# A step loop of an LSTM: the input's gate rows put into the sum by TensorE instead of added behind it

## What is computed

```python
def _lstm_activate(gates, c):
    i, f, g, o = jnp.split(gates, 4, axis=-1)
    c_new = jax.nn.sigmoid(f) * c + jax.nn.sigmoid(i) * jnp.tanh(g)
    h_new = jax.nn.sigmoid(o) * jnp.tanh(c_new)
    return (h_new, c_new)
def step(carry, x_t):
    h, c = carry
    logits = concatenate([h, c, x_t]) @ W_sel.T + b_sel
    s = argmax(logits)
    g = x_t @ W_ih[s].T + h @ W_hh[s].T + b_ih[s] + b_hh[s]
    h2, c2 = _lstm_activate(g, c)
    return ((h2, c2), h2)
```

## Time and profile before

| what | value |
|---|---|
| runs | 6276.47, 6270.70, 6274.82 us; median 6274.8 |
| the profiled execution | 6278.15 us, its span 6276.3 us |
| PE busy | 5392.8 us (86% of the span), 84948 instructions |
| DVE busy | 3097.9 us (49%), 13265 instructions |
| ACT, POOL busy | 1088.6 us (17%), 612.9 us (10%) |
| L1456, gate products | 59904 instructions, 1233.0 us |
| L1427, products that nobody reads | 4992 instructions, 1297.0 us |
| L1480, reductions | 1872 instructions, 670.0 us |
| L1486, additions of the input | 1872 instructions, 416.0 us |

### The profile page before, as it was taken

One profiled execution on the slowest core, in us unless ns is written; L12 is line 12 of the kernel. 1 busy time (PEld: TensorE's weight loads), 2 busy tenths in 40 slices (PEclk: granted clock), 3 DMA queues, 4 the chain that ended last, 5 costly groups with the idle time before them and its releaser, 6 DMA issues. The chain is left out here.

```text
span 6276.3 us, 214043 instructions
## 1 busy us (share of the span) xinstructions
PE 5392.8 (86%) x84948; PEld 3269.5 (52%) x84948; DVE 3097.9 (49%) x13265; ACT 1088.6 (17%) x4645; POOL 612.9 (10%) x1014
## 2 busy tenths in 40 slices
PE   8998778849998929999999999999999999977778
PEld 6643443314666615555555555555555555544444
DVE  4401443214552165555555555555555555564543
ACT  0000000002331131111111111111111111122312
POOL 0000660002650000000000000000000000011100
PEclk9999998979999969999999999999999999989877
DMA  0000111467432330000000000000000000000010
GB/s 10 21 30 11 39 44 44 97 136 253 119 105 100 139 123 5 5 5 10 5 5 5 10 5 5 5 5 10 5 5 5 5 10 0 0 24 37 23 55 9
DMA packets 128787, 240.28 MB, mean 38 GB/s; under 512 B 47084, under 2 KB 64114, under 8 KB 127687
## 3 DMA queue, kind: packets, MB, share of 16 engines
q1 hardware_dynamic: 68584, 146.72, 6.6%
q0 software_dynamic: 60128, 92.58, 5.9%
HBM read 165.58 MB, written 73.29 MB: 38 GB/s over the span
## 5 line engine op out<-in xcount | busy, mean ns | idle before, releaser
L1456 PE MATMUL bank<-lstm_w,step_h_parts 128*32 128x128 f16 (+1 forms) x59904 | 1233.0, 238 | 172.1 <-issue 164.0
L1456 PEld LDWEIGHTS bank<-lstm_w,step_h_parts 128*32 128x32 f16 x59904 | 1116.8, 97 | 488.4 <-issue 478.0
L1427 PE MATMUL bank<-lstm_w 128*128 128x512 f16 x4992 | 1297.0, 383 | 3.2 <-issue 3.2
L1480 DVE TRANSPOSE_TENSOR_REDUCE step_summed<-bank 128x4 f32<-128x128 f32 x1872 | 670.0, 358 | 292.7 <-PE bank L1456 285.6
L1427 PEld LDWEIGHTS bank<-lstm_w 128*128 128x128 f16 x4992 | 386.4, 98 | 388.5 <-issue 5.1
L1406 ACT ACTIVATE step_act_out<-step_gates 128x4 f32<-128x4 f32 x625 | 128.5, 206 | 2082.3 <-DVE step_gates L1486 2078.8
L1486 DVE SCALAR_TENSOR_TENSOR step_gates<-step_summed,lstm_inv_scale,step_xgs 128x4 f32<-128x4 f32 x1872 | 416.0, 222 | 68.7
L1530 DVE COPY step_xgs<-step_xg 128x16 f32 x624 | 109.2, 175 | 688.7 <-issue 664.5
L1396 POOL COPY xnT<-step_state 128x4 f32 (+1 forms) x625 | 116.4, 186 | 3170.0 <-DVE step_state L1513 3170.0
L1109 PE MATMUL bank<-sum_parts,sum_hot 125*125 125x512 f16 x1600 | 347.6, 381 | 6.9 <-DVE sum_parts L1068 6.9
L1437 PE MATMUL bank<-lstm_wsel,step_state 128*1 128x4 f32 x4992 | 214.9, 168 | 115.3 <-DVE step_state L1503 115.3
(11 more groups left out here) (368 smaller groups left out, 6578.2 us busy)
## 6 DMA issues: line engine op xcount, KB each, us to landing
rel_h<-rel_h_sb SPq DMA_DIRECT2D x39, 1024.0 KB, 4.3
lstm_xg<-xg_g POOLq DMA_DIRECT2D x4, 5000.0 KB, 19.5
step_xg<-lstm_xg SPq DMA_DIRECT2D x25, 800.0 KB, 4.4
xg_w<-in_c_w_ih SPq DMA_DIRECT2D x8, 2048.0 KB, 10.7
lstm_w<-in_c_w_hh SPq DMA_DIRECT2D x4, 4096.0 KB, 30.8
rel_z<-rel_z_sb POOLq DMA_DIRECT2D x8, 1250.0 KB, 22.9
rel_zg<-rel_z POOLq DMA_DIRECT2D x8, 1248.0 KB
cheb_w<-in_L_gnn_weight SPq DMA_DIRECT2D x8, 1024.0 KB
```

The source lines that it names most:

```text
L1427: nc.tensor.matmul(idle[:], w[:, 0, 0, 0, 0, 0:128], w[:, 0, 0, 0, 0, :], start=True, stop=True)
L1456: last = nc.tensor.matmul(bank[32 * q:32 * q + 32, 0:32 * (end - first)], h_parts[:, c, :], w[:, s, c, q, a, 32 * first:32 * end], start=( ...
L1480: nc.vector.tensor_reduce(summed[:, first:end], bank[:, 0:32 * (end - first)].rearrange("p (b r) -> p b r", r=32), X_AXIS, ALU.add, apply_ ...
```

## The change

It does four things.

1. `lstm_inputs` is turned: tiles of 125 steps by 512 gate values (16 groups of gate and cell, five tiles each, 80 in all), four products of 512 columns each. ScalarE and VectorE split each tile into three bf16 parts (high, middle, low), whose sum is the fp32 value; GpSimd stores each tile (three parts, 375 rows of 1 KB). The sum of the biases is split in the same way and stored once. The 16 weight loads have 1 MB.
2. In the loop there are four banks, one per gate, each with a column range per cell. For each gate TensorE runs one product (`inject`): a constant 0/1 matrix times the scale as stationary operand, the ring row of the step as moving operand (48 rows of inputs, 48 of biases, 512 columns). It starts the bank's sum; the gate products of the picked cell (128, all of 128 columns) are added to it. The rows for f and g are put in at the top of the loop, those for i and o behind the score products, in front of the wait for the pick. The additions L1486, the row copy L1530 and the buffer `gates` go; ScalarE reads `summed` and multiplies by `L.inv`. VectorE's reductions read the bank at a column offset taken from the pick.
3. `keep_clock_up` and all its products go.
4. VectorE's loop is `choose(t)` and then `finish(t)`, so that its jump back lies between h and the maximum. Four semaphores of the banks are counted down in `choose`. The wait for `h_kept` moves from in front of the cell state to in front of h. The input ring has three slots of five steps.

The diff, without the declarations and the bias splitting:

```diff
-CHUNK = 25
-RING = 3 * CHUNK
-
+GATES = 4
+XG_CHUNK = 5
+XG_SLOTS = 3
+XG_RING = XG_SLOTS * XG_CHUNK
+XG_ROWS = GATES * 4 * 3
...
-    B.xg = nc.dram_tensor("lstm_xg", (CELLS, 128, STEPS * GC), F32, kind="Internal").ap()
...
+    B.xg = nc.dram_tensor("lstm_xg", (GROUPS, 3, STEPS, 512), BF16, kind="Internal").ap()
...
-            for s in range(CELLS):
-                pool.wait_ge(kept_a, GC * (s + 1))
-                pool.wait_ge(kept_v, GC * (s + 1))
-                pool.dma_start(B.xg[s], g[:, s % 2].rearrange("p t g -> p (t g)")).then_inc(stored[s % 2], 16)
-            for i in range(2):
-                pool.wait_ge(stored[i], 16 * (CELLS // 2))
+            for i in range(TILES):
+                n, m = i // NT, i % NT
+                pool.wait_ge(lo_ready, i + 1)
+                pool.dma_start(B.xg[n, :, m * R:(m + 1) * R, :].rearrange("a t g -> t a g"), parts[:, i % 8]
+                               ).then_inc(stored[i % 8], 16)
+            for k in range(8):
+                pool.wait_ge(stored[k], 16 * (TILES // 8))
 
...
+            for i in range(TILES):
+                n, m = i // NT, i % NT
+                if m == 0:
                     pe.wait_ge(w_loaded[n % 2], 16 * (n // 2 + 1))
-                if i >= 4:
-                    pe.wait_ge(kept_a, i - 3)
-                    pe.wait_ge(kept_v, i - 3)
+                if i >= 6:
+                    pe.wait_ge(rest_ready, i - 5)
                 for c in range(KC):
-                    wt = w[:, n % 2, c, i % (GC // 2), :]
-                    nc.tensor.matmul(B.bank[2 * (i % 4)][:, 0:CUT], wt, xnT[:, c, 0:CUT], start=(c == 0),
-                                     stop=(c == KC - 1))
-                    last = nc.tensor.matmul(B.bank[2 * (i % 4) + 1][:, 0:N - CUT], wt, xnT[:, c, CUT:N],
+                    last = nc.tensor.matmul(B.bank[i % 6][0:R, :], xnT[:, c, m * R:(m + 1) * R], w[:, n % 2, c, :],
                                             start=(c == 0), stop=(c == KC - 1))
...
+    part_f = (0, B.bank[0], done_f, summed_f)
+    part_g = (1, B.bank[1], done_g, summed_g)
+    part_i = (2, B.bank[2], done_i, summed_i)
+    part_o = (3, B.bank[3], done_o, summed_o)
+    parts = (part_f, part_g, part_i, part_o)
+    score = B.bank[4][0:1, 0:8]
+    halves = [(c, a) for c in range(KC) for a in range(2)]
     with ExitStack() as here:
-        xg = sb("xg", [128, CELLS, RING * GC], F32)
-        xgs = sb("xgs", [128, GC], F32)
+        xg = sb("xg", [128, XG_RING, 512], BF16)
...
+            def load(k, slot):
+                sp.dma_start(xg[0:XG_ROWS, bass.ds(slot * XG_CHUNK, XG_CHUNK), :],
+                             xg_rows[:, bass.ds(k * XG_CHUNK, XG_CHUNK), :]).then_inc(xg_loaded, 16)
+
+            sp.dma_start(rows_f[:], I["c_xg_rows"]).then_inc(rows_loaded, 16)
+            sp.wait_ge(cleared, 1)
+            sp.dma_start(xg[64:64 + XG_ROWS, :, :], bias_rows.to_broadcast((XG_ROWS, XG_RING, 512))
+                         ).then_inc(bias_loaded, 16)
+            for slot in range(XG_SLOTS):
+                load(slot, slot)
+                sp.wait_ge(xg_loaded, 16 * (slot + 1))
+            with sp.Fori(XG_SLOTS, STEPS // XG_CHUNK) as k:
                 sp.wait_ge(init, 1)
                 sp.wait_ge(xg_loaded, k * 16)
-                sp.wait_ge(xgs_ready, (k - 2) * CHUNK)
-                sp.dma_start(xg[:, :, bass.ds((k % 3) * (CHUNK * GC), CHUNK * GC)],
-                             B.xg[:, :, bass.ds(k * (CHUNK * GC), CHUNK * GC)].rearrange("s p g -> p s g")
-                             ).then_inc(xg_loaded, 16)
-            sp.wait_ge(xg_loaded, STEPS // CHUNK * 16)
+                sp.wait_ge(injected, (k - (XG_SLOTS - 1)) * XG_CHUNK - 1)
+                load(k, k % XG_SLOTS)
 
...
-                act.wait_ge(gates_f, n)
-                nc.scalar.activation(act_out[:, 0:4], gates[:, 0:4], ACT.Sigmoid).then_inc(sig_f, 1)
-                act.wait_ge(gates_ig, n)
-                nc.scalar.activation(act_out[:, 4:8], gates[:, 4:8], ACT.Sigmoid).then_inc(sig_i, 1)
-                nc.scalar.activation(act_out[:, 8:12], gates[:, 8:12], ACT.Tanh).then_inc(tanh_g, 1)
+                act.wait_ge(summed_f, n)
+                nc.scalar.activation(act_out[:, 0:4], summed[:, 0:4], ACT.Sigmoid, scale=L.inv[:, 0:1]
+                                     ).then_inc(sig_f, 1)
+                act.wait_ge(summed_g, n)
+                nc.scalar.activation(act_out[:, 4:8], summed[:, 4:8], ACT.Tanh, scale=L.inv[:, 0:1]
+                                     ).then_inc(tanh_g, 1)
+                act.wait_ge(summed_i, n)
+                nc.scalar.activation(act_out[:, 8:12], summed[:, 8:12], ACT.Sigmoid, scale=L.inv[:, 0:1]
+                                     ).then_inc(sig_i, 1)
                 if ahead:
                     nc.scalar.copy(input_score[:], L.lx[:, bass.ds(n * CELLS, CELLS)]).then_inc(input_score_ready, 1)
-                act.wait_ge(gates_o, n)
-                nc.scalar.activation(act_out[:, 12:16], gates[:, 12:16], ACT.Sigmoid).then_inc(sig_o, 1)
+                act.wait_ge(summed_o, n)
+                nc.scalar.activation(act_out[:, 12:16], summed[:, 12:16], ACT.Sigmoid, scale=L.inv[:, 0:1]
+                                     ).then_inc(sig_o, 1)
                 act.wait_ge(c_ready, n)
                 nc.scalar.activation(tc[:], state[:, 0:4], ACT.Tanh).then_inc(tc_ready, 1)
 
...
-            def keep_clock_up(products):
-
-                for _ in range(products):
-                    nc.tensor.matmul(idle[:], w[:, 0, 0, 0, 0, 0:128], w[:, 0, 0, 0, 0, :], start=True, stop=True)
+            def inject(part, at, stop):
+                p, bank, _, _ = part
+                return nc.tensor.matmul(bank[:], rows[:, p, :], xg[:, at, :], start=True, stop=stop)
+
+            def add_half(part, s, c, a, stop):
+                p, bank, _, _ = part
+                for q in range(4):
+                    last = nc.tensor.matmul(bank[32 * q:32 * q + 32, 128 * s:128 * s + 128], h_parts[:, c, :],
+                                            w[:, s, c, q, a, 128 * p:128 * p + 128], start=False, stop=stop,
+                                            tile_position=(0, 32 * q))
+                return last
+
+            def cell(s):
+                for part in parts:
+                    for c, a in halves:
+                        last = add_half(part, s, c, a, stop=(c == KC - 1 and a == 1))
+                    last.then_inc(part[2], 1)
 
             pe.wait_ge(init, 1)
+            pe.wait_ge(rows_ready, 1)
+            pe.wait_ge(bias_loaded, 16)
+            pe.wait_ge(xg_loaded, 16)
+            for part in parts:
+                inject(part, slice(0, 1), stop=True).then_inc(part[2], 1)
             with pe.Fori(1, STEPS) as t:
 
-                pe.wait_ge(init, 1)
-                pe.wait_ge(input_score_ready, t)
+                pe.wait_ge(xg_loaded, (t // XG_CHUNK + 1) * 16)
+                at = bass.ds(t % XG_RING, 1)
+                for part in (part_f, part_g):
+                    pe.wait_ge(part[3], t)
+                    inject(part, at, stop=False)
+                pe.wait_ge(input_score_ready, 1)
+                pe.sem_inc(input_score_ready, -1)
                 nc.tensor.matmul(score[:, 0:CELLS], B.ones[0:1, 0:1], input_score[:], start=True, stop=False)
                 pe.wait_ge(c_ready, t)
                 for k in range(KC):
@@ -1441,25 +1506,13 @@
                     last = nc.tensor.matmul(score[:, 0:CELLS], tc[:, k:k + 1], h_weight[:, :, k], start=False,
                                             stop=(k == KC - 1))
                 last.then_inc(score_done, 1)
-                keep_clock_up(WARM_PICK - 1)
-                pe.wait_ge(init, 1)
+                for part in (part_i, part_o):
+                    pe.wait_ge(part[3], t)
+                    last = inject(part, at, stop=False)
+                last.then_inc(injected, 1)
+                pe.wait_ge(picked, 1)
                 pe.wait_ge(h_lo_ready, t)
-                keep_clock_up(1)
-                pe.wait_ge(picked, 1)
                 s = pe.value_load(pick[0:1, 0:1])
-
-                def cell(s):
-                    for first, end, bank, done, _, _ in parts:
-                        for c in range(KC):
-                            for a in range(2):
-                                for q in range(4):
-                                    last = nc.tensor.matmul(
-                                        bank[32 * q:32 * q + 32, 0:32 * (end - first)], h_parts[:, c, :],
-                                        w[:, s, c, q, a, 32 * first:32 * end],
-                                        start=(c == 0 and a == 0), stop=(c == KC - 1 and a == 1),
-                                        tile_position=(0, 32 * q))
-                        last.then_inc(done, 1)
-
                 with pe.If(s < 2):
                     with pe.If(s < 1):
                         cell(0)
@@ -1470,22 +1523,14 @@
```

(71 more changed lines are left out.)

159 lines of the change are left out of this document (88 added, 71 removed).

## The result

The changed kernel takes 6345.7 us in the median (6331.6 to 6365.0, 4 runs) where the kernel before takes 6274.6: ratio 1.0116, 95% interval 1.0082 to 1.015. It is slower by 71 us. The profiled execution took 6358.2, 12.5 over that median, with a span of 6356.4, 80.1 longer than before.

The account below looks back on a forecast made before the run. The prediction took the LSTM loop's serial chain, 5.16 us a step, as the bound. Steps gain 0.20 us and lose 0.39 to the clock: 624 x (-0.20 + 0.39) = +119, plus 6 around the loop, gives 6400 us; range 6145 to 6550.

Parts of the forecast that it names:

- the likeliest case: Whole kernel: TensorE's clock falls to half in some loop steps; 6400 us, own range 6240 to 6540, chance 0.52.
- Up to the state: Loop step, first gate product to cell state: 3.02 us falls to 2.47, a gain of 0.55 us a step.
- rival 4: Input additions weren't on the path, the jump back eats the rest, clock full: 6275 +- 12 us, chance 0.06.
- (a): Wait for kept h moves from cell state to new h, beside the tanh wait: 0.07 us, ends 0 and 0.09.
- (b): VectorE's jump back now on the path: maximum at least 0.37 us after the last half of h, before 0.08.
- (c): VectorE loses input-row copy and arithmetic, gains four decrements; reduction of f stays at about +0.8 to 1.0 us, hidden.
- (d): Score products already end before the maximum, so VectorE's jump back is last unless TensorE is late.
- rival 3: TensorE late with the score, 0.15 us a step: 6568 us with half clock in 0.3 of steps, 6250 full; chance 0.12.
- The clock: TensorE in the loop: half clock strikes 0.23 of the steps at 1.7 us each, +0.39 us a step.
- Rival 1: Clock stays full, four row products doing what eight dummies did: 6156 us, chance 0.30.
- The loop's end: Old profile after the last cell: TensorE idle 1.42 us, then half clock; taken as evidence that thin stretches lower the clock.
- Around the loop: Input stage, its stores, the loop's start and first passes: +6 us in sum, ends -15 and +25.

Follow-up runs that it names:

- two steps a pass: Changed kernel with VectorE's loop holding two steps between jumps back, TensorE and ScalarE unchanged: 6267.5 us.
- the wait alone: Changed kernel plus four dummies before the pick's wait (6241.2 us), with VectorE's wait for h_kept moved ahead of the reduction of f: 6222.9 us.
- the kernel with all of it mended: Changed kernel with all rows behind the score, h_kept wait ahead of f's reduction, two dummies directly behind the cell, eight steps per VectorE pass: 5953.0 us, ratio 0.948.

## Why the prediction came out as it did

The direction, the likeliest case and its mechanism were right: 6400 was forecast, 6345.7 came. Two terms of the sum were off, one by +50 us (the jump) and one by -94 (the clock). That the miss is 54 us and not 94 is luck: they partly cancelled.

- **Up to the state: right.** Reduction of o forecast at +2.04 and measured at 2.02, state +2.47 and 2.45 (means over the undisturbed steps; 2.21 and 3.03 before). The additions of the input had been on the path, so rival 4 is out; that is read from the traces, as no run takes them out alone. One price was left out: the scale of the activations, now a column in memory, holds 0.036 us of the path, hidden in a term that came out right.
- **(a) The wait for the kept h: right.** Forecast 0.07, measured 0.509 - 0.434 = 0.075; moving the wait took it away.
- **(b) The jump back: mechanism right, too small.** Forecast 0.37 from the last half of h to the maximum, measured 0.469 in every undisturbed step. The price was read from the old loop, where branch and first instruction behind it stood 0.19 us apart; in the new one they stand 0.30 apart, in every pass. Why the same kind of jump has different prices in the two loops no run shows. It is +0.10 a step, less the 0.02 by which the state came earlier: this is why the full-clock step is 5.04 and not 4.96, 50 us.
- **(c), (d):** the four decrements are hidden, as forecast. TensorE isn't last, but only just: with the jump gone, the maximum waits for the score and comes only 0.1 us earlier (two steps a pass showed it). So rival 3's late score exists, hidden behind the jump.
- **The clock: mechanism right, share and price too large.** Forecast 0.23 of the steps at 1.7 us each, +0.39 a step; measured 101 / 623 = 0.16 at 1.48, +0.24. That is 94 us less. The step from 4022.47 above costs the forecast's 1.70, the one from 4036.02 only 1.22 (6.26 us): there the clock fell after the cell had begun, and its reduction of f isn't late. The share was called the number that no row gives, and four dummies in place of eight in the old kernel, where the same amount streams, gave 148 of 623.
- **Rival 1 and the warning of gaps:** the clock didn't stay full. The largest idle gap of TensorE in the undisturbed step above is 0.79 us, the largest in all the loop's steps 1.36, and 101 steps had half clock all the same. The Trainium skill (TensorE: Matmul & The Clock Gate, Why this matters for your kernels) warns of longer gaps than these; read the other way round, as the prediction read it, that without them the clock stays full, it doesn't hold here. The loop's end, where the clock had fallen after 1.42 us, was the better witness.
- **Around the loop: right within 3 us.** The input stage's products run from 1902.4 to 2179.3, where they ran from 1909.1 to 2180.8: they start 6.7 us earlier (forecast 5) and take 5.2 longer (forecast 6), and the stage's tail is 2 shorter (forecast 5). So the next stage starts 3.5 us earlier (forecast 4), and the loop starts 9.7 later against that (forecast 10).
- **Instruction store:** the two instruction queues of the page of the profile moved 43 and 34 packets in the whole execution, 45 and 30 before, so nothing was reloaded from step to step. With the size that the Trainium skill (Runtime: NRT & Kernel Launch, Instruction fetch mechanics) gives for TensorE's store this agrees.

Terms: 624 x (+0.08 - 0.15) = -44 us and -3 around it, against 125 forecast: 78, the profiled difference of 80.

## What to carry to other kernels

Before dummy products are removed because real ones have come, count what TensorE streams between its dense bursts before and after, and run the old kernel with that many dummies: it prices the clock alone, in one run. Here it gave 141 us for the 150 of the changed kernel, though the number of half-clock steps and the price of one each came out otherwise (148 at 0.95, 101 at 1.48). When an operation is moved across a loop's end, the jump back moves onto the path with it (0.38 us here); holding a few steps in a pass takes it off again, as long as the code stays loaded (eight steps were fine, twelve cost 2.9 us a pass). And where two or three chains stand within 0.1 us of each other, mending one alone shows almost nothing: 18 us for the wait alone, 322 for the kernel with all of it mended.
